# Sixteen token tiles to a loop body, an unrolled SyncE list, and two small operations moved or reshaped, in a fused two-block kernel on one Trainium2 core

## The reference, cut to what matters

```python
# DIM = 128, DEPTH = 6, HEADS = 16, DIM_HEAD = 64, WINDOW = 32, DIM_INNER = 341
def attn_layer(x, Wqkv, qs, ksc, Wo):
    q, k, v = heads(jnp.split(x @ Wqkv, 3, -1))
    q = l2norm(q) * qs                    # t / maximum(norm(t), 1e-12)
    k = l2norm(k) * ksc
    q = q * cos * scale + rotate_half(q) * sin * scale
    k = k * cos / scale + rotate_half(k) * sin / scale
    return local_attention(q, k, v) @ Wo  # a window of 32 and the one before it, softmax

def ffn_layer(x, g, bln, W1, b1, W2, b2):
    xn = (x - mu) / jnp.sqrt(var + 1e-05) * g + bln
    a, gate = jnp.split(xn @ W1 + b1, 2, -1)
    return a * gelu(gate) @ W2 + b2

for i in range(DEPTH):                    # shift_tokens: half of the channels come from the token before
    x = attn_layer(shift_tokens(x), ...) + x
    x = ffn_layer(shift_tokens(x), ...) + x
```

## Time and profile before

| | |
|---|---|
| median of 3 runs | 6615.09 us (6614.57 to 6616.69) |
| profiled execution, its own time | 6612.73 us |
| its span | 6610.9 us |
| mean granted TensorE clock | 0.88 |
| TensorE busy in the span | 5118.0 us |
| VectorE, ScalarE, GpSimd busy | 4022.1, 3052.2 and 2655.6 us |

### The profile page before, as it was taken

How to read it: one execution, slowest core, us unless ns; L and a number is a source line. 1 busy time by engine, 2 the same in 40 slices (tenths; PEclk the granted TensorE clock), 3 DMA queues, 4 the chain that set the end, 5 groups by cost and what they waited for, 6 DMA issues and landing times. The chain is left out here.

```text
span 6610.9 us, 172137 instructions
## 1 busy us (share of the span) xinstructions
PE 5118.0 (77%) x73958; PEld 3242.9 (49%) x74006; DVE 4022.1 (61%) x5250; ACT 3052.2 (46%) x4513; POOL 2655.6 (40%) x1366
## 2 busy tenths in 40 slices
PE   4749999999999999999999994888896444444446
PEld 3326666666666666666666662544543222122234
DVE  3167777777777777777877773233333544444554
ACT  1225555555555555555555552333333333343245
POOL 0025555555555555555555551111011444434400
PEclk9669999999999999999999996788887777777778
DMA  0010001001000100100010000000000000000000
GB/s 21 0 39 15 17 16 37 16 18 27 26 15 18 30 22 17 28 23 18 17 32 19 18 17 9 3 2 2 2 1 7 2 2 2 2 2 1 0 14 18
DMA packets 168396, 94.51 MB, mean 14 GB/s; under 512 B 122170, under 2 KB 155843, under 8 KB 167747
## 3 DMA queue, kind: packets, MB, share of 16 engines
q1 hardware_dynamic: 167747, 84.17, 4.6%
HBM read 23.75 MB, written 3.67 MB: 4 GB/s over the span
## 5 line engine op out<-in xcount | busy, mean ns | idle before, releaser
L930 POOL TENSOR_TENSOR tf_qk<-tf_qk,tf_rot 128x1024 f32<-128x1024 f32 x384 | 909.8, 2369 | 1425.5 <-DVE tf_rot L1299 1425.4
L985 PE MATMUL tf_psum<-tf_Wqkv,tf_xsT 128*128 128x512 f32 x1536 | 762.8, 620 | 116.6 <-issue 74.6
L1878 PE MATMUL mb_psum<-mb_read,ident 128*128 128x512 f32 x512 | 376.5, 883 | 604.3 <-POOL mb_read L1812 604.3
L937 POOL TENSOR_TENSOR tf_qk<-tf_qk,tf_rn 128x1024 f32<-128x1024 f32 x384 | 726.3, 1912 | 125.3 <-ACT tf_rn L1183 125.3
L1812 POOL TENSOR_TENSOR mb_read<-mb_state,mb_Csb 128x512 f32<-128x512 f32 x256 | 396.0, 1574 | 657.4 <-DVE mb_state L2029 644.5
L1176 ACT ACTIVATE tf_sq<-tf_psum 128x1024 f32<-128x1024 f32 x384 | 393.6, 1025 | 449.3 <-DVE tf_rot L1299 448.8
L1295 DVE TENSOR_TENSOR tf_qk<-tf_psum,tf_table 128x1024 f32<-128x1024 f32 x384 | 467.5, 1218 | 167.5 <-PE tf_psum L985 167.5
L1878 PEld LDWEIGHTS mb_psum<-mb_read,ident 128*128 128x128 f32 x512 | 130.4, 278 | 755.8 <-POOL mb_read L1812 636.8
L1058 PE MATMUL tf_psum<-tf_probT,tf_V 32*64 32x64 f32 (+1 forms) x27648 | 490.0, 219 | 4.4 <-issue 3.4
L985 PEld LDWEIGHTS tf_psum<-tf_Wqkv,tf_xsT 128*128 128x128 f32 x1536 | 271.0, 194 | 418.6 <-issue 408.5
L1299 DVE TENSOR_TENSOR tf_rot<-tf_psum,tf_table 128x1024 f32<-128x1024 f32 x384 | 466.2, 1214 | 0.0
(11 more groups left out here) (297 smaller groups left out, 9600.4 us busy)
## 6 DMA issues: line engine op xcount, KB each, us to landing
tf_zr<-z SPq DMA_DIRECT2D x96, 128.0 KB, 2.5
z<-tf_z SPq DMA_DIRECT2D x48, 256.0 KB, 3.0
tf_Wqkv<-in_Wqkv_split SPq DMA_DIRECT2D x18, 512.0 KB, 3.9
tf_zu<-z SPq DMA_DIRECT2D x97, 64.0 KB
tf_zu<-z SPq DMA_DIRECT2D x97, 63.5 KB
tf_zsh<-tf_z SPq DMA_DIRECT2D x96, 64.0 KB
tf_zsh<-tf_z SPq DMA_DIRECT2D x96, 63.5 KB
tf_Wo<-in_L_ffn_Wo SPq DMA_DIRECT2D x6, 512.0 KB, 3.9
```

Source lines behind the costliest of these rows:

```text
L930: nc.gpsimd.tensor_tensor(v, v, rot[:, kind, :], ALU.add).then_inc(added.sem, 1)
L937: nc.gpsimd.tensor_tensor(v, v, rn[:, t, HEADS * kind:HEADS * (kind + 1)].unsqueeze(2) .to_broadcast([P, HEADS, HD]), ALU.mult).then_inc(n ...
L985: last = nc.tensor.matmul(proj[:, half, :], xsT[:, step.unit(0), WIN + t * P:WIN + (t + 1) * P], Wqkv[:, c:c + 512], start=True, stop=True)
L1878: last = nc.tensor.matmul(y_ps[:, :], k.ident[:, :], read[:, m % 2, j, :, :], start=(m == 0 and j == 0), stop=(m == STEPS - 1 and j == 1), ...
```

## The change

1. **Loop body of sixteen steps.** `STEPS8 = 8` becomes `LOOP = 16`: sixteen steps in full, a loop of sixteen steps run 11 times, sixteen steps in full at the end, of which those past the last tile hold only what is left. All positions are worked out from `LOOP`.
2. **SyncE's list.** The loops in each layer are gone; `unit(U)` and `residual(U)` are called for all 96 units with constants. The DMAs and their order stay.
3. **The norms' maximum.** `ss` has two places for each norm, of which the second holds 1e-24. `clamp` is a `tensor_reduce` with max over the pairs of places (one input, 128x32x2 to 128x32 in a new tile `ssc`) in the place of a `tensor_tensor` of `ss` and `least`.
4. **Layer norm's rows on GpSimd.** The four `scalar_tensor_tensor` on VectorE (128x128 each) become two `tensor_tensor` on GpSimd, 128x512 each: subtract the mean, then multiply by the reciprocal deviation, both read with a broadcast. They stand in step 0's GpSimd list between the additions for q and for k.
5. **Order in the steps with ff == 3.** TensorE: `widen(step, 2)` moves behind `scores`, and `output` behind the projection of k. ScalarE: `gelu` of the third block and the table preload move behind the square of q. VectorE: `gate` of the third block moves behind `centre`, and `add_output` behind the rotary embedding of k.

The core of the diff (the other hunks put `LOOP` in place of `STEPS8`, 4 or 2 in the positions):

```diff
-STEPS8 = 8
-ROUNDS = TILES // STEPS8
+LOOP = 16
+ROUNDS = TILES // LOOP
...
-            def unit(G, i, later, pair, change=None, layer=None, first=False):
...
+            def unit(U):
                 nonlocal loads
+                l, i, J = U // B, U % B, U // 2 - 2
+                if i == B - 1 and l + 1 < DEPTH:
                     sp.wait_ge(roped.sem, roped.at(U * 2 + 1, 1))
+                    load_columns(l + 1, 0)
+                    load_table(l + 1, 0)
                     loads += 2
                     sp.wait_ge(weights, 16 * loads)
                 sp.sem_inc(q_ok.sem, 1)
+                if i == B - 1 and l + 1 < DEPTH:
                     sp.wait_ge(roped.sem, roped.at(U * 2 + 1, 2))
+                    load_columns(l + 1, 1)
+                    load_table(l + 1, 1)
                     loads += 2
                     sp.wait_ge(weights, 16 * loads)
                 sp.sem_inc(k_ok.sem, 1)
+                if i == 0 and l:
                     sp.wait_ge(v_done.sem, v_done.at(U * 2 - 1, 1))
+                    load_columns(l, 2)
                     loads += 1
                     sp.wait_ge(weights, 16 * loads)
+                if U:
                     sp.sem_inc(v_ok.sem, 1)
+                if U + 2 <= UNITS:
+                    sp.wait_ge(filled, place(Step(U * 2 // LOOP, U * 2 % LOOP + 1), "input") + 1)
+                    load_input((i + 2) % B)
+                if i % 2 and J >= 0:
+                    save_pair(J % (B // 2), J)
+                    if i == 3 and l:
+                        load_ff_weights(l)
                         loads += 4
                         sp.wait_ge(weights, 16 * loads)
                     sp.sem_inc(ff_ok.sem, 1)
+            def residual(U):
                 nonlocal loads
+                shift_output(U - 2, (U - 2) % 4)
+                load_residual(U % B, U % 2)
+                if U % B == 1:
+                    load_out_weights(U // B)
                     loads += 1
                     sp.wait_ge(weights, 16 * loads)
                 sp.sem_inc(out_ok.sem, 1)
+            for U in range(UNITS):
+                if U >= 2:
+                    residual(U)
+                unit(U)
...
+            def normalise_rows(J):
+                wide = lambda x: x.unsqueeze(2).to_broadcast([P, 4, P])
+                pool.wait_ge(ln_rstd.sem, ln_rstd.at(J, 1))
+                nc.gpsimd.tensor_tensor(xn[:, :, :], zsh[:, :, :], wide(moments[:, :, 0]), ALU.subtract)\
+                    .then_inc(xn_centred.sem, 1)
+                pool.wait_ge(xn_centred.sem, xn_centred.at(J, 1))
+                nc.gpsimd.tensor_tensor(xn[:, :, :], xn[:, :, :], wide(rstd[:, :]), ALU.mult).then_inc(xn_ready.sem, 1)
+
             def body(step):
                 if step.has(1):
                     normalise(step, 0)
                     normalise(step, 1)
                 if step.has(0):
                     rope(step, 0)
+                if step.k % 4 == 0 and step.has_pair():
+                    normalise_rows(step.pair())
+                if step.has(0):
                     rope(step, 1)
                 if step.has(2):
                     weigh(step)
...
                     project(step, 0)
                 if ff == 1:
                     turn_xn(step)
-                elif ff == 3:
-                    widen(step, 2)
                 if step.has(2):
                     scores(step)
+                if ff == 3:
+                    widen(step, 2)
                 if step.has(3):
                     turn_probs(step)
-                if step.has(4):
+                if step.has(4) and ff != 3:
                     output(step)
                 if step.has(0):
                     project(step, 1)
+                if step.has(4) and ff == 3:
+                    output(step)
                 if step.has(1):
                     turn_part(step, 0)
...
-                if ff == 3:
-                    gelu(step.pair(), 2)
-                if ff is not None and ff in (2, 3):
+                if ff == 2:
                     nc.scalar.preload_act_table_set('natural_log_exp_and_others')
                 if ff == 0:
                     inverse_deviation(step.pair())
...
                     copy_xn(step)
                 if step.has(0):
                     square(step, 0)
+                if ff == 3:
+                    gelu(step.pair(), 2)
+                    nc.scalar.preload_act_table_set('natural_log_exp_and_others')
                 if step.has(3):
                     copy_probs(step)
...
-            nc.vector.memset(least[:, :], 1e-24).then_inc(masks_ready, 1)
+            nc.vector.memset(ss[:, :, :, 1:2], 1e-24).then_inc(masks_ready, 1)
...
-                nc.vector.tensor_reduce(ss[:, t, HEADS * kind:HEADS * (kind + 1)],
+                nc.vector.tensor_reduce(ss[:, t, HEADS * kind:HEADS * (kind + 1), 0],
...
-                nc.vector.tensor_tensor(ss[:, t, :], ss[:, t, :], least[:, :], ALU.max).then_inc(clamped.sem, 1)
+                nc.vector.tensor_reduce(ssc[:, t, :], ss[:, t, :, :], AX.X, ALU.max).then_inc(clamped.sem, 1)
...
-            def normalise(J):
-                dve.wait_ge(ln_rstd.sem, ln_rstd.at(J, 1))
-                for s in range(4):
-                    last = nc.vector.scalar_tensor_tensor(out=xn[:, s, :], in0=zsh[:, s, :], scalar=moments[:, s, 0:1],
-                                                          in1=rstd[:, s:s + 1].to_broadcast([P, P]), op0=ALU.subtract,
-                                                          op1=ALU.mult)
-                last.then_inc(xn_ready.sem, 1)
...
                     statistics(step.pair())
                 if step.has(0):
                     rope(step, 0)
+                if step.has(2):
+                    centre(step)
                 if ff == 3:
                     gate(step.pair(), 2)
-                if step.has(2):
-                    centre(step)
-                if step.has(4):
+                if step.has(4) and ff != 3:
                     add_output(step)
                 if step.has(0):
                     sum_squares(step, 0)
                     rope(step, 1)
+                if step.has(4) and ff == 3:
+                    add_output(step)
                 if step.has(2):
                     denominator(step)
                 if step.has(0):
                     sum_squares(step, 1)
                     clamp(step)
-                if ff == 0:
-                    normalise(step.pair())
-                elif ff == 1:
+                if ff == 1:
                     gate(step.pair(), 0)
                 elif ff == 2:
                     gate(step.pair(), 1)
                 elif ff == 3:
-                    add_hidden(step.pair(), step.k // 4)
+                    add_hidden(step.pair(), step.k // 4 % 2)
 
             all_steps(dve, body)
```

More of the change, by code:

```diff
@@ L605, in tile @@
     def tile(self, lag):
-        return self.I * STEPS8 + (self.k - lag)
+        return self.I * LOOP + (self.k - lag)
     def t(self, lag):
@@ L615, in unit @@
     def unit(self, lag):
-        return (self.k - lag) % STEPS8 // TT
+        return (self.k - lag) % 8 // TT
     def has(self, lag):
@@ L625, in pair @@
     def pair(self):
-        return self.I * 2 + (self.k // 4 - 2)
+        return self.I * (LOOP // 4) + (self.k // 4 - 2)
     def has_pair(self):
@@ L632, in before @@
     def before(self):
-        return Step(self.I, self.k - 1) if self.k else Step(self.I - 1, STEPS8 - 1)
+        return Step(self.I, self.k - 1) if self.k else Step(self.I - 1, LOOP - 1)
     def fills(self):
@@ L651, in fill_tables @@
     count, first = 1, {}
-    for k in range(STEPS8):
+    for k in range(LOOP):
         for name in Step(0, k).fills():
@@ L888, in residual @@
                 sp.sem_inc(out_ok.sem, 1)
[L890 to L904, removed]
-                    residual(G + 3, i, 12 + i)
-                    unit(G + 3, i, later, (7 + i) // 2 if i % 2 else None, "qk" if more and i == 3 else None, l + 1)
+            for U in range(UNITS):
+                if U >= 2:
+                    residual(U)
+                unit(U)
             for i in range(2):
@@ L916, in _ @@
         def _(pool):
-            for e in (added, normed, prob_ready):
+            for e in (added, normed, prob_ready, xn_centred, xn_ready):
                 e.start(pool)
@@ L993, in project_v @@
                 if t == 0:
-                    pe.wait_ge(v_ok.sem, v_ok.at(step.I * 4 + (step.k // 2 - 1), 1))
+                    pe.wait_ge(v_ok.sem, v_ok.at(step.I * (LOOP // 2) + (step.k // 2 - 1), 1))
                 pe.wait_ge(centred.sem, centred.at(tau, 1))
@@ L1077, in output @@
                 if t == 0:
-                    pe.wait_ge(out_ok.sem, out_ok.at(step.I * 4 + (step.k // 2 - 2), 1))
+                    pe.wait_ge(out_ok.sem, out_ok.at(step.I * (LOOP // 2) + (step.k // 2 - 2), 1))
                 mixed_free(step)
@@ L1147, in body @@
                 if step.has_input():
```

(6 more changed lines are left out.)

36 lines of the change are left out of this document (7 added, 29 removed).

## The result

6408.24 us (median of 4, 6392.53 to 6414.66) against 6614.83 us: 0.9686 of the kernel before, 95% interval 0.9667 to 0.9705. That is 207 us, where 162 were forecast. The changed kernel measured once more (e12) gave 0.9695. The profiled execution took 6392.53 us, 16 us less than the median: against the profile of before it is 220 us shorter, 207 of them in the changed stage, 6 ahead of it and 7 behind it.

What follows compares the result with a forecast made beforehand. TensorE's own work was taken to bound the kernel, so only its waits count. Loop ends 49, rows 57, inputs 29 and ff == 3 27 sum to 162 us: 6453 us forecast, range 6408 to 6512.

Steps and rivals of the forecast that it cites:

- TensorE's own work sets the pace, and only its waits count: Inside a step TensorE is busy 14.70 of 14.70 us; shortening another engine's operation gains only what it takes off TensorE's waits.
- Loop ends, 49 us: Twelve loop ends fewer, each 2.36 us of TensorE standing idle plus 1.71 us of lower clock, 4.07 us together.
- The rows, net 57 us: Layer norm's rows moved to GpSimd remove TensorE's 1.30 us wait per pair: 59 us, less some 2 in the last pairs.
- the maximum through the inputs, 29 us: Clamp ends 1.6 us earlier, so keep_v and copy_input come earlier and TensorE's 0.6 us wait per input goes.
- ff == 3, 27 us: Reordering and earlier gate remove a 1.07 us wait; a new one of 0.5 for add_output; 48 steps, bounds 0 and 49.
- An issue wait inside the body, no change: TensorE's 23.4 us in 23 waits before transposes depend on where code pieces end; between minus 23 and plus 23 us.
- SyncE's list, nothing: Same DMAs in the same order with constants; no TensorE wait for SyncE seen; bounds minus 5 and plus 5 us.
- rival 4: Late add_output delays layer norm's input through SyncE's DMAs, holding VectorE's statistics: slower; with anything else slower, chance 0.05.
- Rival 1: Fetching costs by amount: TensorE stops inside the longer body (6502), or VectorE and ScalarE stop at loop ends (6453 to 6481); 0.12.
- Rival 2: In ff == 3 the new wait for add_output eats the 27 us gain: 6480, or 6505 with late copies; chance 0.11.
- Rival 3: The maximum as a reduction is stretched beside GpSimd too; 53 us come back, 6506 us; chance 0.05.

Runs made afterwards that it cites:

- e12: The changed kernel itself measured again, on the same chip as e9: 6406.72 us, 0.9695.
- e4: Changed kernel with layer norm's rows as four operations on VectorE again, at the end of step 0's list: 6592.27 us, 0.9973.
- e1: Kernel before with only the body of sixteen steps and SyncE's written-out list: 6565.83 us, 0.9934.
- e2: Changed kernel with a loop body of eight steps, SyncE's list still written out: 6456.86 us, 0.9761.
- e3: Changed kernel with the maximum as a two-input tensor_tensor again: 6495.2 us, 0.9828.
- e13: Changed kernel with 128 long-satisfied waits ahead of TensorE's sixteen steps in full: 6389.26 us, 0.9662.
- e14: Changed kernel with 256 long-satisfied waits ahead of TensorE's sixteen steps in full: 6390.23 us, 0.9669.
- e9: Changed kernel with SyncE's q_ok and k_ok signals and a new layer's q-column and table loads ahead of the residual part: 6390.8 us, 0.9675.
- e5: Changed kernel with the order of the kernel before in steps with ff == 3, on TensorE, ScalarE and VectorE: 6382.29 us, 0.9671.
- e7: Changed kernel with both the two-input maximum and the rows on VectorE as before; sixteen-step body and new order stay: 6575.7 us, 0.9958.
- e15: e9 with the order of the kernel before in steps with ff == 3: 6381.23 us, 0.9659.
- e11: e10 with a loop body of 96 steps: 6344.3 us, 0.9605.
- e10: e9 with the sum of q's squares behind add_output in VectorE's list in steps with ff == 3: 6372.1 us, 0.9651.

## Why the prediction was right in direction and short in size

The step that failed is the price of a wait: the sum took each wait of TensorE at its listed idle time. Measured from start to start, the waits for rows, input and gate cost 0.1 to 0.2 us more each, 14 to 28 us in all. Two terms that the sum had at nothing or too small add to it: the issue waits inside the body fell by 16 us, and the exchange of waits in ff == 3 was worth 32 us of listed time where 27 stood. Two go the other way: the loop ends' term was some 6 us too large, and waits for SyncE took 9 us. The rest of the difference of 45 us stays open, as the sum below shows. The rule has a second flaw, which e4 shows: a wait that gets longer can bring the lower clock behind it, and that is in no listed wait either.

- **TensorE's own work sets the pace, and only its waits count.** Right. VectorE's 442 us of saved work appear nowhere as such. TensorE's listed idle time in the stage fell by 154 of the 207 us.
- **Loop ends, 49 us.** Right in kind and a little large: e1 gave 44, e2 50, and the traces give 43. The prediction counted 24 and 12 loop ends; the stops are 22 and 10, with the same difference. They stand still for 53.2 us before and 27.0 after. The clock fell behind 18 of the 22 and behind 7 of the 10. From the projection's start to that of the output projection it is 4.67 us in a step without a stop; behind all stops together it is 30.4 us more than that before and 13.3 after. So a stop brought 1.38 us of lower clock on average, not 1.71: the row that the prediction used shows one of those where it fell. The gain is 26 + 17 = 43 us.
- **The same kernel twice.** The changed kernel's granted mean was 0.881 in the first profile and 0.878 in e12, where the projections run from 428.4 to 3733.8 us, 11.7 us longer. Of these, 2.6 us are lower clock behind the loop ends and 6.9 behind the five waits for SyncE, behind none of which it fell in the first profile. The first profile is of the shortest execution of that kernel.
- **The rows, net 57 us; the maximum through the inputs, 29 us; ff == 3, 27 us.** The listed waits moved nearly as forecast. For the rows it is 65.8 us in the whole stage before and 8.2 after: 57.6, with 1.7 us lost in the last pair, where 2 were forecast. For the input's copy 30.2 us are gone. For the gate it is 53.9 before and 4.9 after, and `add_output` rose from 0.9 to 18.3: 31.6 net. GpSimd's two operations took 1.04 us each, where 1.1 were forecast.
- **What the listed idle time leaves out.** It is seen at the rows. From the start of the projection of q the rows' transposes start 1.82 us later now. In the kernel before it is 3.28 us, from the start in this line to 2053.46:

```profile
2050.18 1.98 PE L985 MATMUL tf_psum<-tf_Wqkv,tf_xsT 128*128 128x512 f32 x4
```

  That is a gain of 1.46 us, of which 1.30 was listed. The missing 0.16 is in the projection's own duration: the profile gives it 1.98 us, and where there is no wait the next group starts 0.16 us before that end. For the input's copy it is 2.50 us from the start of `widen` to that of the projection before and 1.71 after, 0.79 with 0.61 listed. For the gate it is 3.10 us from 2011.14 to the start in this line, with 1.22 listed:

```profile
2014.24 1.95 PE L1103 MATMUL tf_psum<-tf_xnT,tf_W 128*85 128x512 f32 x4 [1.22 <-DVE tf_hT L1366]
```

  A projection with no wait behind it takes 1.72 to 1.82, so the gate was worth 1.28 to 1.38. At 0.1 to 0.2 us each, the 139 waits of three kinds are worth 14 to 28 us more. e3 points the same way, 94 us against the 53 of the rule, though its issue waits grew too (transposes and scores 36.4 us against 20.8).
- **An issue wait inside the body, no change.** Wrong by about 16 us: on transposes, scores, output and attention 23.4 + 8.9 + 7.5 + 3.4 = 43.2 us before, 12.3 + 8.5 + 6.5 = 27.3 after. e13 and e14 show that it depends on where the code lies, so this part is luck: no edit aimed at it.
- **SyncE's list, nothing.** The list itself costs nothing that was seen, but the later `add_output` does, through SyncE: 9.2 us of waits in the first profile, and about 16 with the clock in e12 against e9. The prediction looked for this in the statistics (rival 4) and it came in a signal that stands in SyncE's list behind a load it has nothing to do with.
- **Rival 1.** Its first form did not happen: 32 steps gain 27 us more. The second did, at a cost that no run shows. The Trainium skill's page Advanced Engine Details and Errata, ISA Cache, gives two lines of 256 instructions; the trace agrees in that VectorE stops at the end of a body of sixteen steps and not of eight, and that the second instruction queue moves 143 packets instead of 35.
- **Rival 2.** In ff == 3 the order shows no gain, by e5, e7 against e1 (0.9958 to 0.9934) and e15: in all three the kernel with the old order is the faster, by 10 to 16 us, each time about as much as the noise and as code that moved can make. Whether the order costs something of its own stays open. The gain that the prediction put there comes from the earlier gate, that is, from the maximum: in e5, with the old order, the gate's wait is 21.9 us instead of 53.9.
- **Rival 3.** Did not happen: 0.22 us. The Trainium skill's rule (SBUF — State Buffer, Who interferes with whom) was right, and e4 shows it once more: three of four two-input operations on VectorE each took 1.8 to 2.0 us beside one of GpSimd's and the fourth 0.34 us behind them. The prediction used it for the operation that goes and not for the rows beside it, one of which was held already before (1987 ns).

By ratios the way from before to after is: loop 0.9934, order 0.9958, rows 0.9828, maximum 0.9686. That is -44, +16, -86 and -94 us, in this order of steps alone, since rows and maximum depend on each other. The last two are known to about 15 us each.

The sum from the profiles is this. Listed waits in the stage: loop ends and start 27.8, rows 57.6, input 30.2, gate and `add_output` 31.6, inside the body 15.9, less 9.2 for SyncE, 154 us. The clock behind loop ends 17. Start to start 14 to 28. Together 185 to 199 us, of the 207 by which the stage got shorter in the first profile and of 196 in that of e12 (3305.4 us long). So 8 to 22 us of the first profile are not accounted for. The start-to-start part of the loop ends and issue waits that went is one candidate; it was not measured. What also stays open is why 96 steps gain no more than 32. The waits for SyncE are not the whole reason: with the signals ahead the step from 16 to 96 was 28 us (e11 against e10), not 41.

## What to carry to other kernels

Price a wait from start to start, against the same two instructions where they run without it, and not by the idle time listed. Where two engines lock each other out, move or reshape all operations of that kind together: one alone can push its neighbour into the lock and lose what it gained. A signal in a hand-written DMA list should stand ahead of every wait that it does not need, and each operation that is moved should be followed into the lists that hang on it.

## What the runs showed that was not expected

- Four row operations of 340 ns each took 5.87 us when they started beside three GpSimd operations in a row; four of the same took 2.77 when three of them came in a gap between GpSimd's operations (e4).
- The lower clock followed TensorE's waits in one execution and not in another of the same kernel: behind four of the five waits of 1.7 to 2.0 us for SyncE in e12 (granted 0.56), behind none of the five in the first profile (1.00).
- 128 satisfied waits ahead of a loop moved TensorE's stops inside it, and the kernel was 0.2 to 0.3% faster.
- VectorE passed the end of an eight-step body without a stop and stopped 2.6 us on average at that of a sixteen-step one.
